# Split weights of the sorted experts made in two passes, the second on ScalarE, and output products moved into the sorted stage

## The chip, the cores and the metric

One core of a Trainium2 chip runs the whole program. The metric is the device time of one execution in microseconds (us). TensorE, VectorE, ScalarE, GpSimd and SyncE run their own instruction streams in order and wait for one another by semaphores; in the views they are PE (PEld for its weight loads), DVE, ACT, POOL and SP.

## What is computed

Sixteen batches of 256 tokens with 128 features go through an attention layer, whose attention matrix also drives a two-layer graph network, and then through a mixture of experts in which each token takes the best two of eight:

```python
attn = softmax(mask(q @ k.T))
out = attn @ v
adj = clip(attn + eye, 0, 1); deg = adj.sum(-1, keepdims=True)
feats = v
for l in range(2):
    feats = gelu(adj @ (feats @ gnn_w[l] + gnn_b[l]) / deg + feats)
x = x + layer_norm((out + feats @ lin_w + lin_b) @ Wo)
...
gate, up = split(normed @ gate_up_weight[e].T)     # 352 columns each, 8 experts
x = x + alpha * sum_e combine[e] * ((silu(gate) * up) @ down_weight[e].T)
```

The last sum runs over the two experts that each token chose.

## The kernel before

**Attention and graph network.** The sixteen batches are worked one after the other by a function `batch` on each engine; batches 0, 1 and 15 are written out, 2 to 14 are a loop. In a batch eight pairs of heads n are worked in a staggered order. That order is written by hand on each engine, as is every wait; nothing is scheduled by a program. One pair's path is: scores on TensorE; `maxima` on VectorE (L1406); `exps` on ScalarE (L1124) into `ea` and `eb`; `adjacency` on VectorE (L1418, L1421), four operations that take the larger of the weights and a scaled identity, with two inputs in SBUF; `weights` on VectorE (L1430); `graph` on GpSimd (L497, L499), which scales `ea` and `eb`; `degrees` on GpSimd (L508); the transposes on TensorE; their copies `gt` on ScalarE; and `differences`, whose result VectorE turns into `aT` (`difference`, `attended`) and ScalarE copies to `gvT`. Then the two graph layers: TensorE's product, VectorE's sum into `z` (`layer1_out`, `layer2_out`, L1455 and L1461), ScalarE's `gelu1`, `gelu2` and the copy `g`. The output products `output_attended` and `output_graph` gather in `bank[7]`; a batch's last seven are made in the next batch, and for batch 15 behind it, ahead of the sorted stage.

**Sorted experts.** Tokens are written to `slots` sorted by expert while later batches run; VectorE makes the table of steps in batch 15 (`table_first`: `passed_by`, `taken`, `used`). Then 71 steps follow, one tile of 128 tokens of one expert each. TensorE transposes the tile (L988), ScalarE and VectorE split it into a rounded high part and a low part (`sz_hi`, `sz_lo`), TensorE makes gate and up with three products for each (high by low, low by high, high by high), ScalarE takes silu, VectorE multiplies into `shid`, TensorE transposes and makes the down product. VectorE's `output_kept` (`y_now`) frees `bank[7]` of batch 15's output.

**The expert weights.** The gate and up weights need the same split, `gu_hi` and `gu_lo`, 128x704 for each of the eight experts. `gu_hi` lies where the attention weights were, so it cannot be written before the last `queries_keys` of batch 15. SyncE loads `raw_gu` into two buffers, the first two loads early and each next one when `gu_lo` of two experts earlier is made. In batch 15 VectorE casts (`gate_up_high`, L1468) behind each `layer2_out`, and GpSimd subtracts (`gate_up_low`, L539) after its last `degrees`.

Of the kernel before, what the change touches and what calls it, by code (L numbers as in the profile page):

```python
# [20 lines left out]
BATCHES, TOKENS, DIM = 16, 256, 128  # L21
# [51 lines left out]
def build_program(nc, x, wq, wk, wv, wvT, gnn_w, gnn_b, lin_wT, lin_b, wo, gamma_in, gamma_out,  # L73
# [10 lines left out]
    with ctx:  # L84
# [75 lines left out]
        gu_lo = sb("gu_lo", [P, EXPERTS, 2 * HID], f32r)  # L160

# [131 lines left out]
        k_gu_hi, k_gu_lo, w_out = sem("k_gu_hi"), sem("k_gu_lo"), sem("w_out")  # L293
# [42 lines left out]
        def _(sp):  # L336
# [95 lines left out]
        def _(pool):  # L432
# [109 lines left out]
            def batch(b, before, routed, after):  # L542

                graph(b, 0)
                degrees(b, 0)
                graph(b, 1)
                degrees(b, 1)
                graph(b, 2)
                degrees(b, 2)
                graph(b, 3)  # L550
                degrees(b, 3)
                graph(b, 4)
                graph(b, 5)
                degrees(b, 4)
# [7 lines left out]
                graph(b, 6)  # L562
                if routed is not None:
# [3 lines left out]
                graph(b, 7)  # L567
                degrees(b, 7)
                if after is not None:
                    deviation(after, 1, 7)  # L570
                if after is None:
                    for e in range(0, 3):
                        gate_up_low(e)
# [4 lines left out]
                if after is None:  # L578
                    for e in range(3, 5):
                        gate_up_low(e)  # L580
                if before is not None:
                    token_power(before, 2)
                if after is None:
                    for e in range(5, EXPERTS):
                        gate_up_low(e)
# [46 lines left out]
        def _(pe):  # L632
# [1425 lines left out]
```

## Time and profile before

| | us |
|---|---|
| median of 3 runs | 1147.88 |
| lowest and highest | 1142.15, 1152.14 |
| the profiled execution | 1155.31 |
| its span, first to last instruction | 1153.4 |

| engine | busy us | share of the span |
|---|---|---|
| TensorE, matmul | 1071.1 | 93% |
| TensorE, weight load | 854.7 | 74% |
| VectorE | 884.1 | 77% |
| ScalarE | 803.4 | 70% |
| GpSimd | 500.3 | 43% |

The profiled execution took 7.4 us more than the median. Batch 1, called the second batch here, runs from 84 to 142 us, the last batch from 898 to 955, the sorted stage from 957 to about 1135. A view by stage gives the busy time of each engine within a stretch and the clock that TensorE was granted; a timeline gives the start, the duration, the engine, the line and the tiles, with the idle time before it and what ended that in brackets. Durations of neighbouring instructions overlap a little, so the step from start to start is shorter than the duration.

### The profile page before, as it was taken

What the parts mean: (1) busy time and instruction counts of PE and PEld (TensorE: products, weight loads), DVE (VectorE), ACT (ScalarE), POOL (GpSimd) and SP (SyncE); (2) the same over time, 40 slices, a digit from 0 to 9 for tenths busy, and PEclk for the clock granted to TensorE, in tenths of its full rate; (3) what the DMA queues carried; (4) which work ended last, traced back from release to release, by engine and by line L of the source; (5) the groups of instructions that cost most, each with busy time, mean ns of one, the idle gap of its engine ahead of it and who ended that gap; (6) DMA issues with size and microseconds to landing.
All of it is one profiled execution on the core that took longest, in us unless ns stands there. A gap on an engine that the chain in (4) does not pass through costs nothing.

```text
span 1153.4 us, 28732 instructions
## 1 busy us (share of the span) xinstructions
PE 1071.1 (93%) x8576; PEld 854.7 (74%) x8576; DVE 884.1 (77%) x3760; ACT 803.4 (70%) x2351; POOL 500.3 (43%) x649
## 2 busy tenths in 40 slices
PE   4899999999999999999999999999999968898993
PEld 3777777777777777777777777777777747898993
DVE  3667797979797979797979797979797984565556
ACT  3668686868686868686868686868787735464551
POOL 3334244434343535353534353535353552544444
PEclk9899999999999999999999999999999988998997
DMA  6970000000000000000000000000000021222227
GB/s 192 405 260 2 1 2 11 1 10 1 10 1 11 1 10 0 10 0 10 0 10 0 10 0 10 0 10 0 10 0 10 2 78 44 56 57 61 59 61 226
DMA packets 37312, 47.43 MB, mean 41 GB/s; under 512 B 6009, under 2 KB 28539, under 8 KB 37200
## 3 DMA queue, kind: packets, MB, share of 16 engines
q1 hardware_dynamic: 32880, 37.81, 10.3%
q0 software_dynamic: 4320, 8.47, 2.2%
q14 instruction: 84, 0.69, 0.2%
q8 instruction: 28, 0.46, 0.2%
HBM read 18.14 MB, written 28.58 MB: 41 GB/s over the span
## 4 chain that ended last, share of the span: by engine, by line
PE 83%; DVE 6%; issue 3%; ACT 2%; SPq 2%; DMA 1%; another core or an unknown queue 1%; POOL 0%; DVEq 0%; POOLq 0%; ACTq 0%
PE bank L635 68%; PE bank L735 3%; PE bank L748 3%; PE bank L774 2%; PE bank L751 2%; PE bank L749 2%; PE bank L1006 2%; DMA x_all<-in_x 1%; PE bank L988 1%; DVE eb L1421 1%; DVE x_all L1995 1%; DVE got L1993 1%; DVE nmax L1406 0%; PE bank L783 0%
## 5 line engine op out<-in xcount | busy, mean ns | idle before, releaser
L497 POOL TENSOR_TENSOR ea<-ea,wgt 128x256 f32<-128x256 f32 x128 | 80.0, 625 | 429.6 <-DVE wgt L1430 396.1
L1406 DVE TENSOR_REDUCE nmax<-bank 128x1 f32<-128x128 f32 (+1 forms) x512 | 152.2, 347 | 66.0 <-PE bank L635 57.1
L499 POOL TENSOR_TENSOR eb<-eb,wgt 128x512 f32<-128x512 f32 x128 | 133.6, 1044 | 0.0
L635 PE MATMUL bank<-gt,g 128*64 128x256 f32 (+1 forms) x1024 | 112.0, 339 | 19.5 <-DVE z L1461 12.0
L1421 DVE SCALAR_TENSOR_TENSOR eb<-idw,ssum,eb 128x256 f32<-128x256 f32 x256 | 129.8, 544 | 0.0
L1124 ACT ACTIVATE ea<-bank,nmax 128x128 f32<-128x128 f32 x256 | 95.8, 374 | 47.9 <-DVE nmax L1406 45.9
L1124 ACT ACTIVATE eb<-bank,nmax 128x256 f32<-128x256 f32 x256 | 123.4, 482 | 0.0
L1092 ACT ACTIVATE gt<-bank 128x512 f32<-128x512 f32 (+1 forms) x256 | 111.7, 493 | 13.3 <-PE bank L751 11.8
L635 PE MATMUL bank<-gt,vnat 128*64 128x256 f32 (+1 forms) x1024 | 110.0, 335 | 3.0 <-issue 0.8
L635 PE MATMUL bank<-qk 64*128 64x128 f32 (+1 forms) x1024 | 112.7, 339 | 0.0
L525 POOL DMA_INDIRECT pairs<-zout,zin x71 | 69.7, 981 | 99.0 <-DVE zout L1954 89.3
L635 PEld LDWEIGHTS bank<-gt,g 128*64 128x64 f32 x1024 | 66.5, 137 | 61.4 <-issue 35.4
L1092 ACT ACTIVATE g<-bank 128x256 f32<-128x256 f32 x128 | 48.8, 381 | 84.8 <-PE bank L635 84.8
L635 PEld LDWEIGHTS bank<-gt,vnat 128*64 128x64 f32 x1024 | 65.1, 136 | 50.2 <-issue 17.0
L1461 DVE TENSOR_TENSOR z<-bank,f1T 128x256 f32<-128x256 f32 x128 | 53.6, 419 | 48.5 <-PE bank L635 48.5
L635 PE MATMUL bank<-xt_lo,w_hi 128*128 128x256 f32 x256 | 87.0, 340 | 1.9 <-DVE xt_lo L1399 1.9
L635 PE MATMUL bank<-gw,f1T 128*128 128x128 f32 x512 | 88.1, 295 | 0.3 <-ACT f1T L1148 0.3
L1947 DVE TENSOR_TENSOR shid<-bank,ssg 128x352 f32<-128x352 f32 x71 | 37.3, 525 | 63.5 <-ACT ssg L1272 40.6
L1092 ACT ACTIVATE qk<-bank 128x512 f32<-128x512 f32 x128 | 78.1, 610 | 11.2 <-PE bank L635 8.9
L635 PEld LDWEIGHTS bank<-gw,f1T 128*128 128x128 f32 x512 | 70.3, 192 | 19.3 <-issue 11.0
L1418 DVE SCALAR_TENSOR_TENSOR ea<-ident,ssum,ea 128x128 f32<-128x128 f32 x256 | 83.2, 362 | 0.0
L1092 ACT ACTIVATE gvT<-bank 128x256 f32<-128x256 f32 x128 | 49.1, 383 | 44.2 <-DVE aT L1440 40.6
(234 smaller groups left out, 3153.0 us busy)
## 6 DMA issues: line engine op xcount, KB each, us to landing
slots<-zero SPq DMA_DIRECT2D x33, 520.0 KB, 15.0
zin<-slots SPq DMA_DIRECT2D x71, 65.0 KB
got<-pairs SPq DMA_DIRECT2D x8, 512.0 KB, 5.5
raw_gu<-in_guT SPq DMA_DIRECT2D x8, 352.0 KB, 3.0
out<-x_all SPq DMA_DIRECT2D x8, 256.0 KB, 2.7
pairs<-zout,zin POOLq DMA_INDIRECT x71
dn<-in_downT SPq DMA_DIRECT2D x2, 512.0 KB, 16.0
slots<-z,row_now POOLq DMA_INDIRECT x64
```

What stands on the lines that cost most here:

```text
L497: nc.gpsimd.tensor_tensor(ea[:, s], ea[:, s], wgt[:, s, 0:2].unsqueeze(2).to_broadcast([P, 2, P]), ALU.mult)
L499: nc.gpsimd.tensor_tensor(eb[:, s], eb[:, s], wgt[:, s, 2:4].unsqueeze(2).to_broadcast([P, 2, 2 * P]), ALU.mult).then_inc(p_g.sem, 1)
L525: nc.gpsimd.indirect_dma_start(pairs, bass.IndirectOffsetOnAxis(ap=zin[:, j % RING, ID:ID + 1].bitcast(u32), axis=0), zout[:, j % RING, :] ...
L635: return nc_mm(o, st, mo, start=first, stop=last, **more)
L735: mm = nc.tensor.transpose(o[:, m * TOKENS + t * P:m * TOKENS + (t + 1) * P], vnat[:, t, n * P:(n + 1) * P], ident[:, :])
L1092: return nc.scalar.activation(o, i, ACT.Copy, **more)
L1124: done = nc.scalar.activation(e[:, s, a, :], score_bank(n, a)[:, TILE_SCORES[t]], ACT.Exp, bias=nmax[:, s, i:i + 1], accum_out=ssum[:, s, ...
L1406: done = V.tensor_reduce(nmax[:, n % 3, i:i + 1], score_bank(n, a)[:, TILE_SCORES[t]], X, ALU.max, negate=True)
L1418: V.scalar_tensor_tensor(ea[:, s, a, :], ident[:, :], ssum[:, s, a:a + 1], ea[:, s, a, :], ALU.mult, ALU.max, accum_out=den[:, s, a:a + 1])
L1421: done = V.scalar_tensor_tensor(eb[:, s, a, :], idw[:, :], ssum[:, s, 2 + a:3 + a], eb[:, s, a, :], ALU.mult, ALU.max, accum_out=den[:, s, ...
L1461: V.tensor_tensor(z2[:, n % 2, :], bank[L2_BANK][:, 0:TOKENS], f1T[:, n % 4, :], ALU.add).then_inc(d_z2.sem, 1)
L1947: V.tensor_tensor(shid[:, j % 2, 0:HID], bank[2 + j % 2][:, 0:HID], ssg[:, j % 2, :], ALU.mult).then_inc(d_hid.sem, 1)
```

## The change

The weight split is made in two passes. In the second batch VectorE casts the raw weights of expert e into `gu_top`, which lies in the buffer `zin` that the sorted stage uses later, right behind `weights(b, e)`; GpSimd subtracts it to make `gu_lo` right behind `graph(b, e)`, ahead of `degrees(b, e)`. There is one `gu_top`, so from the second expert on VectorE waits for GpSimd's subtraction before. All raw weights are then loaded a second time, and ScalarE casts them to `gu_hi` in the last batch, behind each `gelu1`. The seven last output products of batch 15 move behind the transposition of the sorted stage's first tile; `output_natural` and `output_kept` move from step 0 to step 1, the wait for `y_now` to step 2; and ScalarE calls a silu of one column ahead of the first slots, so that the table for silu is loaded there.

```diff
+        gu_top = zin[:, :, :].rearrange("p r d -> p (r d)")[:, 0:2 * HID].bitcast(f32r)
...
+            for e in range(EXPERTS):
+                if e < 2:
+                    sp.wait_ge(k_gu_lo, EXPERTS - 1 + e)
+                else:
+                    sp.wait_ge(k_gu_hi, e - 1)
+                sp.dma_start(raw_gu[:, e % 2, :], guT[e]).then_inc(w_gu[e % 2], 16)
...
             def gate_up_low(e):
-                pool.wait_ge(k_gu_hi, e + 1)
-                nc.gpsimd.tensor_tensor(gu_lo[:, e, :], raw_gu[:, e % 2, :], gu_hi[:, e, :].bitcast(f32),
+                pool.wait_ge(k_gu_top, e + 1)
+                nc.gpsimd.tensor_tensor(gu_lo[:, e, :], raw_gu[:, e % 2, :], gu_top.bitcast(f32),
                                         ALU.subtract).then_inc(k_gu_lo, 1)
...
+            def output_rest():
+
+                output_attended(BATCHES - 1, 5)
+                output_attended(BATCHES - 1, 6)
+                output_graph(BATCHES - 1, 4)
+                output_graph(BATCHES - 1, 5)
+                output_graph(BATCHES - 1, 6)
+                output_graph(BATCHES - 1, 7)
+                output_attended(BATCHES - 1, PAIRS - 1)
...
                 slots_transposed(0)
+                output_rest()
                 d_zlo.wait(pe, 0, 1)
                 slots_transposed(1)
...
                 pe.wait_ge(k_gu_lo, EXPERTS)
+                pe.wait_ge(k_gu_hi, EXPERTS)
...
-                    if j == 0:
+                    if j == 1:
                         output_natural(last)
+                    if j == 2:
                         d_y.wait(pe, last, 1)
...
+            def gate_up_high(e):
+                act.wait_ge(w_gu[e % 2], 16 * ((EXPERTS + e) // 2 + 1))
+                if e == 0:
+                    s_qk.wait(act, BATCHES - 1, PAIRS)
+                copy(gu_hi[:, e, :], raw_gu[:, e % 2, :]).then_inc(k_gu_hi, 1)
...
             def sorted_stage():
+                nc.scalar.activation(warm[:, :], half[:, 0:1], ACT.Silu)
                 slots_high(0)
...
-            def gate_up_high(e):
+            def gate_up_top(e):
                 dve.wait_ge(w_gu[e % 2], 16 * (e // 2 + 1))
-                if e == 0:
-                    s_qk.wait(dve, BATCHES - 1, PAIRS)
-                V.tensor_copy(gu_hi[:, e, :], raw_gu[:, e % 2, :]).then_inc(k_gu_hi, 1)
+                if e >= 1:
+                    dve.wait_ge(k_gu_lo, e)
+                V.tensor_copy(gu_top, raw_gu[:, e % 2, :]).then_inc(k_gu_top, 1)
...
                 slots_low(0)
+                output_bias(BATCHES - 1)
                 slots_low(1)
-                output_bias(BATCHES - 1)
...
-                    if j == 0:
+                    if j == 1:
                         output_kept(BATCHES - 1)
```

GpSimd at the start of the second batch, pairs 0 and 1, before (`ea` and `eb` are the scaled attention weights, `deg` the degrees):

```order
L497 TENSOR_TENSOR ea<-ea,wgt 128x256
L499 TENSOR_TENSOR eb<-eb,wgt 128x512
L508 TENSOR_TENSOR deg<-den,rs 128x256
L497 TENSOR_TENSOR ea<-ea,wgt 128x256
L499 TENSOR_TENSOR eb<-eb,wgt 128x512
L508 TENSOR_TENSOR deg<-den,rs 128x256
```

and in the changed kernel, where `zin` is the name of the buffer in which `gu_top` lies:

```order
L504 TENSOR_TENSOR ea<-ea,wgt 128x256
L506 TENSOR_TENSOR eb<-eb,wgt 128x512
L546 TENSOR_TENSOR gu_lo<-raw_gu,zin 128x704
L515 TENSOR_TENSOR deg<-den,rs 128x256
L504 TENSOR_TENSOR ea<-ea,wgt 128x256
L506 TENSOR_TENSOR eb<-eb,wgt 128x512
L546 TENSOR_TENSOR gu_lo<-raw_gu,zin 128x704
L515 TENSOR_TENSOR deg<-den,rs 128x256
```

One subtraction of 704 columns stands in each pair between `eb` and `deg`; for all eight pairs it is so.

VectorE at the same place in the changed kernel, from the `weights` of pair 0 (`wgt`) to the cast behind that of pair 1; before, the same rows stood without the two casts to `zin`:

```order
L1473 RECIPROCAL wgt<-den 128x4
L1511 CAST zin<-raw_gu 128x704
L1449 TENSOR_REDUCE nmax<-bank 128x1 x4
L1459 RECIPROCAL rs<-ssum 128x4
L1461 SCALAR_TENSOR_TENSOR ea,den<-ident,ssum,ea 128x128 x2
L1464 SCALAR_TENSOR_TENSOR eb,den<-idw,ssum,eb 128x256 x2
L1473 RECIPROCAL wgt<-den 128x4
L1511 CAST zin<-raw_gu 128x704
```

The cast stands between `wgt` and the maxima of the next pair, and the adjacency's four operations follow those.

ScalarE in the last batch of the changed kernel, around the second and third `gelu1` (`f1T`), where before the same rows stood without the casts to `gu_hi`:

```order
L1112 ACTIVATE gt<-bank 128x256
L1168 ACTIVATE f1T<-z,gb 128x256
L1112 ACTIVATE gu_hi<-raw_gu 128x704
L1112 ACTIVATE gvT<-bank 128x256
L1168 ACTIVATE f1T<-z,gb 128x256
L1112 ACTIVATE gu_hi<-raw_gu 128x704
L1112 ACTIVATE g<-bank 128x256 x2
L1112 ACTIVATE gt<-bank 128x512
```

These are the casts of experts 1 and 2; that of expert 0 stands two rows ahead of these, behind the first `f1T`. The copies `g`, for which the second layer's products wait, stand behind the third cast.

## Rows read from the trace of the kernel before

**Rows 1.** Busy time by stage: stretch, its length, busy of PE, PEld, DVE, ACT, POOL, clock.

```profile
84.00:142.00 58.00, 56.58 (x473) 43.82 (x471) 44.00 (x195) 45.20 (x135) 20.93 (x29) 1.00 0.01 1
926.00:955.00 29.00, 18.86 (x110) 13.40 (x107) 23.80 (x56) 8.78 (x22) 16.54 (x15) 0.76 0.31 86
```

**Rows 2.** The chain that ended last, in order of time: start, us, what.

```profile
926.20 4.40 DVE passed_by L1837
...
944.97 0.43 DVE gu_hi L1468
```

**Rows 3.** The tile `raw_gu`: durations in ns min/median/max, first and last start.

```profile
L1468 DVE CAST gu_hi<-raw_gu x8: 511/516/527, 923.5 to 953.9; 128x704 fp32r<-128x704 f32 x8
L539 POOL TENSOR_TENSOR gu_lo<-raw_gu,gu_hi x8: 1655/1672/1786, 928.8 to 954.5; 128x704 fp32r<-128x704 f32 x8
...
DMA to landing us min/median/max: 2.9/3.0/6.9
```

**Rows 4.** Timeline of the last batch, VectorE and GpSimd.

```profile
922.23 0.42 DVE L1813 TENSOR_TENSOR taken<-used,tile_to 128x256 f32<-128x256 f32 x1
...
928.85 1.66 POOL L539 TENSOR_TENSOR gu_lo<-raw_gu,gu_hi 128x704 fp32r<-128x704 f32 x1
...
942.26 1.67 POOL L539 TENSOR_TENSOR gu_lo<-raw_gu,gu_hi 128x704 fp32r<-128x704 f32 x1 [2.28 <-DVE gu_hi L1468]
...
942.36 1.86 DVE L1702 TENSOR_TENSOR x_all<-x_all,t 128x256 f32<-128x256 f32 x1
...
946.12 1.07 DVE L1713 TENSOR_SCALAR ve<-ss 128x2 f32<-128x2 f32 x1
...
948.20 1.78 DVE L1813 TENSOR_TENSOR taken<-used,tile_from 128x256 f32<-128x256 f32 x1
```

**Rows 5.** Timeline of the second batch, three engines.

```profile
118.58 1.04 POOL L499 TENSOR_TENSOR eb<-eb,wgt 128x512 f32<-128x512 f32 x1
118.64 1.13 DVE L1418 SCALAR_TENSOR_TENSOR ea<-ident,ssum,ea 128x128 f32<-128x128 f32 x1
...
122.65 1.66 DVE L1668 TENSOR_SCALAR t<-y_now,mv,rs 128x128 f32<-128x128 f32 x2
...
125.97 0.87 PE L635 MATMUL bank<-gt,g 128*64 128x256 f32 x8 [1.18 <-DVE z L1461]
```

**Rows 6.** Timeline of VectorE in the second batch.

```profile
95.41 0.18 DVE L1430 RECIPROCAL wgt<-den 128x4 f32<-128x4 f32 x1
...
98.13 0.32 DVE L1418 SCALAR_TENSOR_TENSOR ea<-ident,ssum,ea 128x128 f32<-128x128 f32 x1
...
99.80 0.17 DVE L1430 RECIPROCAL wgt<-den 128x4 f32<-128x4 f32 x1
...
121.80 0.16 DVE L1430 RECIPROCAL wgt<-den 128x4 f32<-128x4 f32 x1
```

**Rows 7.** Timeline of GpSimd in the second batch: start, us, instruction, [idle before].

```profile
95.67 0.61 POOL L497 TENSOR_TENSOR ea<-ea,wgt 128x256 f32<-128x256 f32 x1 [2.60 <-DVE wgt L1430]
96.24 1.04 POOL L499 TENSOR_TENSOR eb<-eb,wgt 128x512 f32<-128x512 f32 x1
97.24 0.61 POOL L508 TENSOR_TENSOR deg<-den,rs 128x256 f32<-128x256 f32 x1
```

**Rows 8.** TensorE's granted clock behind its long wait, columns as in the first group.

```profile
931.50:933.00 1.50, 1.50 (x9) 0.86 (x9) 1.02 (x6) 0.29 (x1) 1.24 (x1) 0.50 0.77 225
```

**Rows 9.** The tile `w_hi`: ScalarE's cast of it, durations in ns.

```profile
L1092 ACT ACTIVATE w_hi<-raw x2: 1056/1056/1057, 5.4 to 6.9; 128x1024 fp32r<-128x1024 f32 x2
```

**Rows 10.** Timeline of TensorE before the long wait of the last batch.

```profile
919.90 0.82 PE L635 MATMUL bank<-gt,g 128*64 128x256 f32 x8
```

**Rows 11.** Timeline of the first steps of the sorted stage.

```profile
959.12 0.42 PE L635 MATMUL bank<-gu_lo,sz_hi 128*128 x1
...
959.46 1.28 ACT L1272 ACT_TABLE_LOAD   x1
...
963.04 0.42 PE L635 MATMUL bank<-gu_lo,sz_hi 128*128 x1 [2.33 <-DVE y_now L1448]
```

More of the change, by code:

```diff
@@ L537, in gate_up_low @@
             def gate_up_low(e):
-                pool.wait_ge(k_gu_hi, e + 1)
-                nc.gpsimd.tensor_tensor(gu_lo[:, e, :], raw_gu[:, e % 2, :], gu_hi[:, e, :].bitcast(f32),
+                pool.wait_ge(k_gu_top, e + 1)
+                nc.gpsimd.tensor_tensor(gu_lo[:, e, :], raw_gu[:, e % 2, :], gu_top.bitcast(f32),
                                         ALU.subtract).then_inc(k_gu_lo, 1)
             def batch(b, before, routed, after):
+                first_pass = before is not None and routed is None
                 graph(b, 0)
+                if first_pass:
+                    gate_up_low(0)
                 degrees(b, 0)
                 graph(b, 1)
+                if first_pass:
+                    gate_up_low(1)
                 degrees(b, 1)
                 graph(b, 2)
+                if first_pass:
+                    gate_up_low(2)
                 degrees(b, 2)
                 graph(b, 3)
+                if first_pass:
+                    gate_up_low(3)
                 degrees(b, 3)
                 graph(b, 4)
+                if first_pass:
+                    gate_up_low(4)
                 graph(b, 5)
+                if first_pass:
+                    gate_up_low(5)
                 degrees(b, 4)
@@ L1211, in batch @@
                 gelu1(b, 0)
+                if after is None:
+                    gate_up_high(0)
                 graph(b, 5)
                 gelu1(b, 1)
+                if after is None:
+                    gate_up_high(1)
                 mixed_values(b, 4)
                 gelu1(b, 2)
+                if after is None:
+                    gate_up_high(2)
                 layer2_in(b, 0)
@@ L1221, in batch @@
                 gelu1(b, 3)
+                if after is None:
+                    gate_up_high(3)
                 gelu2(b, 0)
                 gelu1(b, 4)
+                if after is None:
+                    gate_up_high(4)
                 gelu2(b, 1)
@@ L1227, in batch @@
                 gelu1(b, 5)
+                if after is None:
+                    gate_up_high(5)
                 layer2_in(b, 4)
@@ L1232, in batch @@
                 gelu1(b, 6)
+                if after is None:
+                    gate_up_high(6)
                 layer2_in(b, 5)
@@ L1239, in batch @@
                 gelu1(b, 7)
+                if after is None:
+                    gate_up_high(7)
                 layer2_in(b, 7)
@@ L1548, in batch @@
                 layer2_out(b, 0)
-                if after is None:
-                    gate_up_high(0)
                 weights(b, 7)
+                if first_pass:
+                    gate_up_top(7)
                 difference(b, 5)
@@ L1563, in batch @@
                 layer2_out(b, 1)
-                if after is None:
-                    gate_up_high(1)
                 if before is not None:
@@ L1572, in batch @@
                 layer2_out(b, 2)
-                if after is None:
-                    gate_up_high(2)
                 difference(b, 6)
@@ L1596, in batch @@
                 layer2_out(b, 4)
-                if after is None:
-                    gate_up_high(4)
                 difference(b, 7)
@@ L1605, in batch @@
                 layer2_out(b, 5)
-                if after is None:
-                    gate_up_high(5)
                 layer1_out(b, 7)
```

43 lines of the change are left out of this document (20 added, 23 removed).

## The prediction

> **What bounds the kernel now.** I read the profile in this order: the busy time by stage, the chain that ended last, the timeline of the second batch, the timeline of the last batch, and the first steps of the sorted stage.
>
> In the second batch (from 84 to 142 us) TensorE is busy 56.58 of 58 us at a full granted clock, VectorE 44.00 and GpSimd 20.93 [rows 1]. TensorE is the bound there, and there is hardly any idle time to lose anything in. In the end of the last batch (926 to 955 us) TensorE is busy 18.86 of 29 us at a mean granted clock of 0.76 and VectorE 23.80 [rows 1]. There VectorE is the bound, and the chain says so: it runs through 4.40 us of `passed_by` and through casts to `gu_hi`, each 0.43 us of it [rows 2]. So the change takes VectorE and GpSimd work from a place where it is on the path, and puts it where TensorE is the bound and has no room. What it costs there decides.
>
> **What the second batch pays.** Eight VectorE casts of 128x704 and eight GpSimd subtractions of the same size go in. A cast takes 516 ns and a subtraction 1672 ns [rows 3]; of the cast 0.43 us stand in the chain [rows 2], the rest overlaps with its neighbours. Summed alone that is 3.4 us on VectorE and 13.4 us on GpSimd, and GpSimd is busy 20.93 of 58 us, so by busy time it would fit.
>
> It does not fit by position. VectorE's operations with two SBUF inputs wait while GpSimd works. In the last batch the 128x64 `passed_by`, in the chain from 926.20 for 4.40 us [rows 2], ended 0.1 us after a subtraction that began at 928.85 and took 1.66; a 128x256 addition to `x_all` took 1.86 us beside a subtraction that began 0.10 us before it; `ve` on 128x2 took 1.07 us, and `taken` 1.78 us against 0.42 for the same form undisturbed [rows 4]. In the second batch the same happens once to the adjacency: an `ea` of 128x128 took 1.13 us, beside a GpSimd `eb` that ended at 119.62 [rows 5], against 0.32 us for one that met nothing [rows 6].
>
> Now the cycle of one pair n there. `weights` ends at 95.59 [rows 6], GpSimd starts 0.08 us later and does `ea`, `eb`, `deg` until 97.85 [rows 7]; the next adjacency begins at 98.13 and its `weights` at 99.80 [rows 6]. The adjacency just misses GpSimd, by 0.28 us. From the second `weights` at 95.41 to the eighth at 121.80 [rows 6] there are six periods, of 4.40 us in the mean. After the change, counted from the end of `weights`: the cast, first in VectorE's order, holds GpSimd back by about 0.3 us; `ea` and `eb` take 0.57 and 1.00 us from start to start [rows 7], the subtraction about 1.64, `deg` 0.57. The subtraction thus ends at 0.1 + 0.3 + 1.57 + 1.64 = 3.6 us and `deg` at 4.2. The next adjacency, due at about 2.5 to 3.0, waits to 3.6. It does one of its four operations (0.25 us), waits for `deg` to 4.2, and does the rest. From its first operation to the next `weights` is 99.80 - 98.13 = 1.67 us now [rows 6], so 4.2 + 1.42 + 0.1 = 5.7 us to the next `weights`, against 4.4. Over seven periods that is 7 x 1.3 = 9.1 us. Behind the last `weights` two normalisations, now 1.66 us with a wait, meet the eighth subtraction too, about 1.6 us more, and TensorE already waits there for VectorE, 1.18 us [rows 5], so this comes through in full. That makes 10.7. I take off 1.7, an estimate, for the first periods, in which VectorE idles for TensorE now: **+9.0 us**. TensorE waits for `gvT` and `z`, both behind the late operations in VectorE's order, and since it is 98% busy it makes nothing good later.
>
> The ends of this price: below, if adjacency and subtraction never meet, only the casts remain, and these partly in idle time: +2 us. Above, if a waiting operation is not let in between two GpSimd instructions (`passed_by` stood behind the whole queue of them), each adjacency waits for `deg` whole, 0.35 us more a period, and nothing is taken off, +13 us. I take the value in between since the `ea` of 1.13 us, the same operation, was let in at the end of `eb`, before `deg`.
>
> The Trainium skill says the same of the mechanism: by "SBUF — State Buffer", section "Who interferes with whom", VectorE and GpSimd share one port pair under an exclusive lock, an instruction of VectorE with two SBUF inputs contends with a GpSimd instruction that reads SBUF, and whoever issues first holds it for its whole instruction. By that rule a waiting operation comes in when the instruction that holds the ports ends, which is the period of 5.7 us and the 9.0; the `ea` of 1.13 us agrees, and `passed_by`, which stood behind several instructions, goes further than the rule and would give the 13.
>
> The raw weights are loaded twice now, eight more transfers of 352 KB. A load lands in 3.0 us [rows 3] and has two periods of over 4 us; that costs nothing in the second batch. GpSimd's `degrees` and powers come up to 1.7 us later; inside the 9.0.
>
> **What the last batch gains.** (a) `passed_by` is released when GpSimd's queue ends without the first subtraction, 928.9 instead of 930.5: **-1.7 us**, as TensorE waits for the `z` behind it. (b) From 937 us to 951 us the chain is VectorE's. Gone are the waits of `x_all` (1.86 to 0.42), `ve` (1.07 to 0.17) and `taken` (1.78 to 0.42) [rows 4], the short times of the first two by their widths, 3.7 us, and three casts of 0.43 us, 1.3 us. With VectorE 5.0 us faster the round from `z2` through TensorE and ScalarE becomes the limit, so I let 1.3 us of it go and count **-3.7 us**. (c) TensorE's granted clock is 0.50, the lower level of 1.2 GHz, at 931.5 to 933 us [rows 8], behind its long idle stretch; its busy part on the chain there is slower than at 2.4 GHz. With that stretch shorter some of it comes back; 0 to 4 us, I take **-1.5 us**.
>
> ScalarE gets eight casts of 128x704. A 128x1024 one took 1056 ns [rows 9], so about 0.79 us each, 6.3 us in all; ScalarE is busy 8.78 of 29 us at the end [rows 1], which hides the last five. The first three stand in a crowded place. The third needs a load that can start only when the first has released its buffer, at about 918.3 us by my estimate, and lands 3.0 us later [rows 3]; ScalarE stands in front of it until 921.3, and `layer2_in` behind it, for which TensorE's `gt,g` products, at 919.90 now [rows 10], wait until about 922.4. That 2.5 us is covered by the wait for `passed_by` until 928.9, and TensorE idles 10 of the 29 us there [rows 1]. Cost nothing; 2.5 us if that cover is gone.
>
> **What the sorted stage gains.** The two slot conversions on ScalarE and VectorE now run under the seven moved products, but a table load of 1.28 us [rows 11] now stands before the first conversion: -0.7 us. Between step 0 (959.12) and step 1 TensorE waits 2.33 us for `y_now` [rows 11]. With the table loaded before and the wait two steps later, step 1 follows directly and the transposition behind it costs nothing: -2.1 us. Together **-2.8 us**, from nothing to 4 us. All later stalls of the stage hang on its step numbers and shift with it.
>
> **Sum.** +9.0 - 1.7 - 3.7 - 1.5 - 2.8 = -0.7 us on the profiled execution, which took 1155.31 us. The median of the timed runs is 1147.88 us, 7 below it, so the sum is put on the median: 1147.2 us.
>
> **Rivals.**
> 1. The port is not the limit in the second batch (+2 us instead of +9). For it: VectorE idles there 14 us by busy time. Against it: the 0.28 us by which the adjacency clears GpSimd now. 1147.9 - 9.7 + 2 = 1140 us.
> 2. Slower: TensorE's waits in the second batch, 1 to 2 us in each period, bring its clock to the lower level as behind the idle stretch at 926 us, and the batch becomes slow on TensorE too. For it: 0.50 at 931.5 [rows 8]. It decides when the clock is down for over 8 us of the batch, since half of that is lost: +4 to +8. Against it: its waits are broken up by work. With `deg` waited for whole it gives 1147.9 + 13 + 4 - 9.7 = 1155 us.
> 3. The gain of the last batch does not come: ScalarE's third cast delays the queue by 2.5 us with no cover, and TensorE's chain is the limit anyway, so that (a) to (c) bring 2 us rather than 6.9: 1152 us.
>
> **How the numbers follow.** The forecast has 0.48, rival 1 has 0.24, rival 2 has 0.14, rival 3 has 0.14. The likeliest gives 1147.2 us, with 1143 to 1151 as its own range. The whole range, to rivals 1 and 2 and their bounds, is 1138 to 1157 us. A measurement of this kernel tells about 1% from no change: under 1136.4 all gains at their upper bounds and the cheap second batch must meet, 0.07; over 1159.4 rival 2 must meet the failing gains, 0.08; 0.85 lies within.
>
> **What would show it.** In the second batch: `weights` to `weights` at 5.7 us, `ea` and `eb` of VectorE over 1 us at each pair, TensorE waiting several times. If `ea` stays at 0.32 to 0.35 us there, the term of 9.0 us is wrong. In the last batch: `passed_by` under 3 us, `x_all`, `taken` and `ve` at their short times, and ScalarE waiting for a load ahead of its third cast. In the sorted stage: no wait for `y_now`, and step 2 about 3.2 us after step 0. A batch two that ends more than 13 us late, or a clock below 1.00 in it, would make the forecast too low.

## The result and the profile after

| | before | after |
|---|---|---|
| median of 6 runs each, us | 1147.82 | 1162.82 |
| lowest and highest | 1142.15, 1152.14 | 1160.69, 1165.88 |
| span of the profiled execution | 1153.4 | 1161.9 |

The ratio is 1.0131, with a 95% interval of 1.0100 to 1.0161: the change costs 15 us. The forecast of 1147.2 us is wrong, and the range, which ended at 1157, too.

Four stretches of the trace that can be cut at the same events in both kernels say where the time went. I cut at the first `weights` of a batch (VectorE's reciprocal into `wgt`), at the first gate and up product and at the last transposition of a hidden tile.

| stretch, us | before | after | difference |
|---|---|---|---|
| second batch, to the first `weights` of batch 2 | 56.9 | 67.5 | +10.6 |
| batches 2 to 14, to the first `weights` of batch 15 | 742.7 | 759.2 | +16.5 |
| last batch, to the first gate and up product | 69.0 | 58.1 | -10.9 |
| sorted stage, to its last transposition | 175.8 | 168.1 | -7.7 |

The differences add up to 8.5 us and not to the 15 of the medians, since the profiled execution of before took 7.4 us more than its median. The first, the third and the fourth are what the prediction was about. The second was in no sentence of it: in the loop of batches 2 to 14 no line was changed, and it costs 16.5 us more, the size of the whole loss. Of the fourth only a part is the change's, as the runs below show.

The views by stage, the second batch first, then the last. The columns are start and end of the stretch, its length, the busy time of each engine with its instructions, TensorE's granted clock, and the DMA share and rate.

```profile
core 0: us, PE busy (x) PEld busy (x) DVE busy (x) ACT busy (x) POOL busy (x), PEclk, DMA share, GB/s
90.50:158.00 67.50, 57.96 (x457) 44.34 (x456) 56.47 (x208) 44.39 (x132) 35.84 (x37) 0.97 0.15 44
917.20:975.30 58.10, 51.66 (x415) 39.03 (x413) 48.58 (x198) 44.56 (x127) 23.88 (x31) 1.00 0.20 52
```

For the same two stretches of the kernel before:

```profile
90.60:147.50 56.90, 55.48 (x459) 42.89 (x458) 44.56 (x201) 43.92 (x133) 20.93 (x29) 1.00 0.01 2
890.10:959.10 69.00, 56.65 (x415) 42.46 (x412) 57.84 (x206) 37.75 (x118) 37.23 (x39) 0.90 0.16 44
```

In the second batch GpSimd has 15 us more and VectorE 12 us more, of which only some 4 us are casts. In the last batch VectorE lost 9 us and GpSimd 13, and TensorE's clock is at its full level (2.4 GHz) throughout, where it was 0.90 in the mean.

How the second batch loses, from the timelines of GpSimd and then of VectorE in the kernel after (start, duration, engine, line, operation, tiles; in brackets the idle time before and what ended it):

```profile
96.86 1.03 POOL L506 TENSOR_TENSOR eb<-eb,wgt 128x512 f32<-128x512 f32 x1
97.85 1.68 POOL L546 TENSOR_TENSOR gu_lo<-raw_gu,zin 128x704 fp32r<-128x704 f32 x1
99.49 0.66 POOL L515 TENSOR_TENSOR deg<-den,rs 128x256 f32<-128x256 f32 x1
...
101.62 0.80 POOL L504 TENSOR_TENSOR ea<-ea,wgt 128x256 f32<-128x256 f32 x1 [1.47 <-DVE wgt L1473]
```

```profile
98.06 1.62 DVE L1461 SCALAR_TENSOR_TENSOR ea<-ident,ssum,ea 128x128 f32<-128x128 f32 x1
99.61 0.08 DVE L1461 DVE_READ_ACCUMULATOR ea<-ident,ssum,ea 128x1 f32 x1
99.61 0.69 DVE L1461 SCALAR_TENSOR_TENSOR ea<-ident,ssum,ea 128x128 f32<-128x128 f32 x1
```

The first `ea` of this pair, 0.32 us long in [rows 6], starts 0.21 us behind the subtraction and ends 0.15 us behind it; the second takes 0.69 us and ends 0.15 us behind `deg`. GpSimd's `ea` of the eight pairs begin at 90.82 to 129.53 us, a period of 5.53 us.

How the loop loses. This is VectorE's timeline at the jump from one pass to the next in the kernel after, and then at the same jump in the kernel before:

```profile
383.60 0.43 DVE L1504 TENSOR_TENSOR z<-bank,f1T 128x256 f32<-128x256 f32 x1 [1.94 <-PE bank L650]
386.81 0.62 DVE L1449 TENSOR_REDUCE nmax<-bank 128x1 f32<-128x128 f32 x2 [2.78 <-PE bank L650]
389.27 0.62 DVE L1449 TENSOR_REDUCE nmax<-bank 128x1 f32<-128x128 f32 x2 [1.84 <-issue]
389.81 0.17 DVE L1773 COPY lg<-bank 128x16 f32<-128x16 f32 x1
```

```profile
369.12 0.42 DVE L1461 TENSOR_TENSOR z<-bank,f1T 128x256 f32<-128x256 f32 x1 [1.95 <-PE bank L635]
372.13 1.15 DVE L1406 TENSOR_REDUCE nmax<-bank 128x1 f32<-128x128 f32 x4 [2.58 <-PE bank L635]
373.19 0.17 DVE L1729 COPY lg<-bank 128x16 f32<-128x16 f32 x1
...
374.59 0.17 DVE L1737 MAX8 top<-lg 128x8 f32<-128x8 f32 x1 [0.35 <-issue]
```

Before, four reductions follow one another (and a small stand of 0.35 us comes 18 instructions behind the head). After, VectorE does two, then stands still for 1.84 us with nothing to wait for ("issue"), and then does the other two of the four. Over all passes, VectorE's waits of after and then TensorE's (in all, times, the longest):

```profile
DVE nmax L1449 <- issue: 23.7, 13, 2.8
```

```profile
PE bank L650 <- DVE lg L1773: 8.9, 12, 0.9
PE bank L750 <- ACT vnat L1112: 3.3, 12, 0.3
```

The loop jumps back twelve times. VectorE's 13 waits are the twelve second stands and once the first one. TensorE waits 0.7 us in the mean for `lg` in each of twelve passes, and 0.3 us for `vnat`; for neither it waited before. From jump to jump a pass takes 58.49 us in the mean against 57.12, 1.37 us more. An engine that stands still at one place in its code, on no semaphore, in every pass, may be waiting for the code itself. The DMA queues on the page show code being read (packets, MB, share), after first:

```profile
q14 instruction: 86, 0.70, 0.2%
q8 instruction: 28, 0.46, 0.2%
```

```profile
q14 instruction: 84, 0.69, 0.2%
q8 instruction: 28, 0.46, 0.2%
```

Their number hardly differs, so it is not that more is read. What differs is when it is needed. In the trace VectorE has 429 instructions ahead of the loop's head before and 444 after: the eight casts and seven waits of the change make it 15 later. The packets of queue 14 are of 8192 bytes (0.70 MB in 86). In both traces a packet of this queue begins 1.0 to 1.2 us behind the jump of VectorE's loop shown, and the next one 0.8 us after VectorE goes on. The theory to test, called P: VectorE's code comes in blocks; behind the jump the block with the head is read, and then the next; after the change only three instructions of the loop stand in the first of them.

### The profile page after: what moved, and what is told of

The parts are those of the page before. It is cut to its first block, busy times and chain, and to the rows that moved or that the text cites. A ratio compares the mean times of both kernels' runs of the same rounds, so it can differ in the third digit from the quotient of the medians.

```text
span 1161.9 us, 28757 instructions
## 1 busy us (share of the span) xinstructions
PE 1073.4 (92%) x8576; PEld 853.1 (73%) x8576; DVE 890.8 (77%) x3760; ACT 812.3 (70%) x2360; POOL 501.4 (43%) x649
## 4 chain that ended last, share of the span: by engine, by line
PE 62%; DVE 19%; issue 10%; DMA 3%; ACT 3%; SPq 2%; POOL 1%; DVEq 1%; ACTq 0%; POOLq 0%
PE bank L650 49%; DVE eb L1464 4%; PE bank L750 3%; DVE nmax L1449 3%; DVE ea L1461 2%; PE bank L789 2%; PE bank L763 2%; DVE z L1498 2%; PE bank L766 2%; PE bank L764 2%; PE bank L1021 2%; DVE z L1504 1%; DMA zin<-slots 1%; DVE dT L1478 1%; DVE t L1712 1%
## 5 line engine op out<-in xcount | busy, mean ns | idle before, releaser
L1461 DVE SCALAR_TENSOR_TENSOR ea<-ident,ssum,ea 128x128 f32<-128x128 f32 x256 | 89.9, 388 | 0.0
```

The lines of the kernel that those rows point to most:

```text
L1461: V.scalar_tensor_tensor(ea[:, s, a, :], ident[:, :], ssum[:, s, a:a + 1], ea[:, s, a, :], ALU.mult, ALU.max, accum_out=den[:, s, a:a + 1])
```

## Experiments

Twelve kernels ran. Times are medians in us, and each group was timed beside the kernel before on its own chip, which differs by up to 8 us from group to group; so only differences and ratios within a group are compared. "The good place" means that VectorE's loop head stands near the start of a block.

| run | time | before beside it | ratio, 95% interval |
|---|---|---|---|
| before, head 15 later | 1168.61 | 1153.38 | 1.0148 (1.0122 to 1.0174) |
| after, head 2 later | 1177.53 | 1153.38 | 1.0215 (1.0185 to 1.0245) |
| after, head 4 later | 1151.68 | 1153.38 | 0.9993 (0.9974 to 1.0013) |
| before with the sorted part | 1148.46 | 1153.38 | 0.9955 (0.9936 to 0.9974) |
| after, head 4 later, subtractions of 2 columns | 1134.90 | 1146.12 | 0.9886 (0.9853 to 0.9919) |
| after, head 4 later, without the sorted part | 1147.86 | 1146.12 | 1.0011 (0.9999 to 1.0023) |
| after, subtractions on VectorE | 1139.22 | 1146.12 | 0.9941 (0.9924 to 0.9959) |
| before with the sorted part, head 19 later | 1140.85 | 1146.12 | 0.9958 (0.9943 to 0.9972) |
| before, head 19 later | 1142.59 | 1145.31 | 0.9981 (0.9964 to 0.9998) |
| the same with the sorted part and ScalarE's casts | 1137.35 | 1145.31 | 0.9927 (0.9911 to 0.9944) |
| after, head 94 later | 1145.88, one run | 1145.31 | |
| after, head 102 later | 1145.0, one run | 1145.31 | |

### Does the place of the loop's head make the 16 us?

The first kernel is before with 15 idle instructions on VectorE ahead of its first wait; each EVENT_SEMAPHORE holds two waits that are satisfied.

```diff
+            for _ in range(30):
+                dve.wait_ge(w_x0, 16)
             dve.wait_ge(w_x0, 16)
             for i in range(5):
```

> The kernel before, with 15 more instructions on VectorE ahead of its first wait: each waits for a semaphore that has its value anyway. Nothing else changes; the loop of batches 2 to 14 stands 15 instructions later in VectorE's code, as in the kernel after. Theory P (place of the loop's head in the code): in the trace of the kernel after, VectorE stands still 1.7 us behind the third instruction of every pass, on no semaphore, and a pass takes 58.5 us against 57.1; so this kernel must show the same stall and passes of 58.4 to 58.6 us, and be 13 x 1.3 = about 16 us slower, 1164 us. Theory C (the second batch's casts and subtractions, or what follows from them, slow the loop down): this kernel has none of them, passes stay at 57.1 us and the time at 1148.

It took 15.2 us more than before, ratio 1.0148, with nothing of the change in it. Its trace at the jump, and its wait over all passes:

```profile
375.94 0.62 DVE L1406 TENSOR_REDUCE nmax<-bank 128x1 f32<-128x128 f32 x2 [2.56 <-PE bank L635]
378.38 0.62 DVE L1406 TENSOR_REDUCE nmax<-bank 128x1 f32<-128x128 f32 x2 [1.82 <-issue]
```

```profile
DVE nmax L1406 <- issue: 23.3, 13, 2.9
```

This is the stall of after at the same instruction, and a pass takes 58.44 us. The second batch keeps its 56.8 us there, so its casts and subtractions are not needed for the slow loop. The other way round, the kernel after with 2 and with 4 more (`range(8)` in the second):

```diff
+            for _ in range(4):
+                dve.wait_ge(w_x0, 16)
             dve.wait_ge(w_x0, 16)
```

> The kernel after with 2 more such instructions on VectorE ahead of its first wait. Theory P with code read in blocks of 128 instructions: the head then stands 1 instruction ahead of a block's end instead of 3, the stall stays, behind the first instruction instead of the third; pass 58.4 us or a little more, time 1163 us. Theory C: no change, 1163 us. It is the partner of the next kernel, which has 2 more.

> The kernel after with 4 more such instructions. Theory P: the loop's head passes the end of a block, so that 127 instructions of the loop are in the first block read behind the jump; the stall of 1.7 us is gone, a pass takes 57.0 us or a little less, and the time is 1163 - 13 x 1.3 to 1.6 = 1142 to 1147 us. Theory C: 1163 us, as the one with 2.

With 2 it is 24 us slower than before, with 4 it is 1.7 us faster than before: two idle instructions are worth 26 us. VectorE's timeline with 2, then with 4:

```profile
385.61 0.43 DVE L1504 TENSOR_TENSOR z<-bank,f1T 128x256 f32<-128x256 f32 x1 [1.94 <-PE bank L650]
391.20 1.15 DVE L1449 TENSOR_REDUCE nmax<-bank 128x1 f32<-128x128 f32 x4 [5.16 <-issue]
```

```profile
379.41 0.43 DVE L1504 TENSOR_TENSOR z<-bank,f1T 128x256 f32<-128x256 f32 x1 [1.94 <-PE bank L650]
381.67 1.15 DVE L1449 TENSOR_REDUCE nmax<-bank 128x1 f32<-128x128 f32 x4 [1.83 <-PE bank L650]
```

With 2 the second stall has moved up to the second instruction, as the theory said. But a pass takes 59.19 us, more than the 58.4 that I had written, and the kernel is 24 us over before where the expectation meant 15; both stands together are 5.16 us, and no reduction of the pass is done between them. Whether that makes the additional 0.7 us of a pass was not tested. With 4 both stalls are gone. VectorE waits 1.83 us for TensorE and for nothing else; a pass takes 57.00 us, and the profile shows

```profile
q14 instruction: 26, 0.21, 0.1%
```

26 packets instead of 86. I had expected that the stall would go, not that all reading would stop. So VectorE can hold the whole loop, but only from some places. Two more kernels test a rule for that, with 94 and with 102 idle instructions.

> The kernel after with 94 more satisfied waits ahead: the loop's head is instruction 90 of its block (from 0), the jump at its end 288 further, in the third block. If four blocks of 128 are held and one is fetched ahead, the block of the head is still there when the loop jumps: no fetch of code in the loop, about 26 packets in the instruction queue, 0.2 us behind the jump. Time as the one with 4, if the waits ahead cost nothing.

> The same with 102: head at 98, the jump in the fourth block, so the next one was fetched over the head's. Fetches in every pass again (84 to 86 packets), 2.7 to 2.9 us from the jump to the next instruction, but no second stall, as 30 instructions are in the first block read. Time within 2 us of the one with 94.

Both came out as written, the times from one run each. The queue and VectorE's timeline with 94, and then with 102:

```profile
q14 instruction: 27, 0.22, 0.1%
```

```profile
381.23 0.43 DVE L1504 TENSOR_TENSOR z<-bank,f1T 128x256 f32<-128x256 f32 x1 [1.94 <-PE bank L650]
383.49 1.15 DVE L1449 TENSOR_REDUCE nmax<-bank 128x1 f32<-128x128 f32 x4 [1.83 <-PE bank L650]
```

```profile
q14 instruction: 87, 0.71, 0.2%
```

```profile
381.53 0.43 DVE L1504 TENSOR_TENSOR z<-bank,f1T 128x256 f32<-128x256 f32 x1 [1.94 <-PE bank L650]
384.51 1.15 DVE L1449 TENSOR_REDUCE nmax<-bank 128x1 f32<-128x128 f32 x4 [2.55 <-PE bank L650]
```

With blocks of 128, a block border ahead of instruction 447 (counted from 0) fits all places: after (head at 444) stalls behind three instructions, with 2 more behind one, and before (429) has its small stand behind 18. With 4 more the head is at 448, one behind the border by this count, not the block's first as I had written, and the jump 288 instructions further is in the third block, counted from the head's; with 94 (538) it is still in the third, with 102 (546) in the fourth. The packets fit a store of four blocks into which the next one is read ahead: with the jump in the fourth block, as also in before and after, the head's block has been written over. This store is worked out from which places read and which don't; no view shows it.

The reading alone costs nothing here: with 102 a pass takes 56.99 us, and with 94, where nothing is read, 56.99 too. At 429 the 18 loop instructions ahead of the border cover the reading of the next block but for 0.35 us. So three cases were seen: no reading; reading whose 2.6 us hide under VectorE's wait for TensorE; and, with 3 or 1 instructions left in the head's block, a second stall that does not hide. How many instructions between 3 and 18 are enough was not tried.

The Trainium skill has this mechanism in "Runtime: NRT & Kernel Launch", section "Instruction fetch mechanics": a taken branch to a page outside the window makes the engine wait for a DMA that brings it. The trace agrees in kind. The page speaks of blocks of 256 instructions; here the measurement decides, and eight kilobytes and 128 instructions fit for VectorE. With borders every 256 instructions through the same 447 the jump of the kernel with 102 would be in the block next to its head's, and it reads in every pass.

What the better place gives a kernel that already had no second stall:

> The kernel before with 19 more satisfied waits ahead, so that the loop's head is the first instruction of a block. Theory P: a pass takes 57.0 us without the spread of 56.95 to 57.66 that the profile of before shows, and the fetches in the loop are gone: 13 x 0.12 = 1.6 us at most, 1144.5 to 1146 us where before is 1146. So the other kernels with this place of the head have at most 1.6 us from it.

2.7 us by the medians, where at most 1.6 was expected; the interval of 0.9964 to 0.9998 (0.2 to 4.1 us) takes that in. A pass takes 56.98 us there, without the slow ones up to 57.66. The loop's stretch in the traces bounds it better: 742.7 us in before, 741.4 in the kernel with the sorted part alone, which has its head at the same place, and 741.1 here. So the good place is worth 0.3 to 1.6 us against that of before.

### What is the change worth without that?

The kernel after with 4 more is the change at a good place: 0.9993 of before, or -0.8 us with -3.0 to +1.5, where the prediction's sum was -0.7. But before stands at a slightly worse place; against before at the good one (0.9981, in another group) it is 1.0012, +1.4 us, with about -1.6 to +4.4 by both intervals together. Either way the change is nothing that these runs can tell from zero. Its parts:

> The kernel before with the sorted stage's part of the change alone: seven output products behind the first transposition, output_natural and output_kept one step later, the wait for y_now two steps later, the table of silu loaded ahead. VectorE's code ahead of the loop is that of before, so passes stay at 57.1 us. By the prediction's term -2.8 us: 1145 us. By the two traces, in which the stretch from the first gate and up product to the last hidden transposition shrank by 7.7 us, up to -7.7 us: 1140 us. If most of that 7.7 us comes from the earlier end of the last batch's work instead (weights split ready earlier), 1145 to 1147 us.

```diff
+                output_rest()
...
-                    if j == 0:
+                    if j == 1:
                         output_natural(last)
+                    if j == 2:
                         d_y.wait(pe, last, 1)
...
+                nc.scalar.activation(warm[:, :], half[:, 0:1], ACT.Silu)
```

4.9 us by the medians (3.0 to 7.4 by the interval), and the wait for `y_now`, 2.33 us in [rows 11], is gone. At the good place the sorted part was run in another group:

> The sorted part alone (e4) with 19 more instructions ahead, which puts the loop's head at the same place as in e3, the first instruction of a block by my count. A pass is 57.00 us there against 57.02 in the profile of e4 and 57.12 in that of before. So it gives 0.2 to 1.5 us on top of e4: 1147 to 1148 us where before is 1153. The fetches of code in the loop disappear (26 packets in the instruction queue instead of 84).

0.9958 with it against 0.9981 without (above, on another chip): 0.23%, 2.6 us, beside a prediction of 2.8. The sorted stage's stretch of the table at the top took 171.3 and 161.3 us in the two kernels with the sorted part alone (head as before, and 19 later), and 168.7 in the one with 19 idle instructions and no sorted part. It moves by 10 us between two kernels, on two chips, that differ only in the place of the loop; in the one of 161.3 the granted clock was 1.00 over the whole stretch, in that of before 0.96. So a part of the -7.7 us of the two profiles is such a difference, and by the times 2.6 to 4.9 us are the change's.

The split of the weights alone, at the good place:

> The kernel after with 4 more instructions ahead, the sorted stage's part undone: the seven output products, output_natural, output_kept, the wait for y_now and silu's table stand as in the kernel before. The split of the weights in two passes is there. By the runs so far the whole change at the good place is -1.7 us and the sorted part alone -4.9, so by addition the split alone is +3 us against before: 1156 us where before is 1153. By the prediction's terms it is +9.0 - 6.9 = +2.1. If the sorted part's gain needs the earlier low parts (the stretch from the first gate and up product shrank by 7.7 us in the whole change), the split alone is worse, +6 us.

```diff
-                output_rest()
+            output_attended(BATCHES - 1, 5)
...
-                    if j == 1:
+                    if j == 0:
                         output_kept(BATCHES - 1)
```

+1.7 us, ratio 1.0011 with 0.9999 to 1.0023, against before at its own place, which is 0.3 to 1.6 us worse by the traces. The prediction's terms give +9.0 - 6.9 = +2.1. The two halves of the split largely cancel, and of the change as written the sorted part is the only clear gain.

### What costs the 10.6 us in the second batch?

> The kernel after with 4 more instructions ahead (the good place of the loop's head), and in the second batch GpSimd subtracts 2 columns of each expert instead of 704; the other columns of the low parts are zero, filled once by GpSimd at 17 us where it idles. So the low parts are left out but for 2 columns. VectorE's eight casts stay. If the second batch's price is GpSimd's 1.67 us holding VectorE's two-input operations, the batch gets back nearly all of its 10.7 us: 3 us at most are left for the casts, the period of weights is 4.4 to 4.6 us, and the time is 8 us under that of the partner with 4 (e3), about 1144 us where that is 1152. If the casts or the loads cost it, under 3 us come back.

```diff
-                nc.gpsimd.tensor_tensor(gu_lo[:, e, :], raw_gu[:, e % 2, :], gu_top.bitcast(f32),
+                nc.gpsimd.tensor_tensor(gu_lo[:, e, 0:2], raw_gu[:, e % 2, 0:2], gu_top[:, 0:2].bitcast(f32),
```

11.2 us under before by the medians, ratio 0.9886, so 12 us under its partner of 0.9993 where 8 were expected; its runs spread over 9 us, and the trace is the surer measure. The second batch takes 57.8 us: of the 10.6 us, 9.7 belong to GpSimd's subtraction and 0.9 to the eight casts and the loads. VectorE's first two adjacency operations of a pair in the second batch, and its casts, in the kernel after and then in this one (busy, mean ns):

```profile
L1461 DVE SCALAR_TENSOR_TENSOR ea<-ident,ssum,ea 128x128 f32<-128x128 f32 x16 | 12.6, 823 | 0.0
L1511 DVE CAST zin<-raw_gu 128x704 fp32r<-128x704 f32 x8 | 4.2, 527 | 0.0
```

```profile
L1463 DVE SCALAR_TENSOR_TENSOR ea<-ident,ssum,ea 128x128 f32<-128x128 f32 x16 | 5.4, 378 | 0.0
L1513 DVE CAST zin<-raw_gu 128x704 fp32r<-128x704 f32 x8 | 4.0, 499 | 0.0
```

823 against 378 ns for 16 of them is 7.1 us of waiting. Another 1.9 us stand in the normalisations of the same stretch: `t` (two of 1279 against 820 ns), `xh` (two of 490 against 335) and `ve` (804 against 168). One of them beside the subtraction, in after:

```profile
119.64 1.67 POOL L546 TENSOR_TENSOR gu_lo<-raw_gu,zin 128x704 fp32r<-128x704 f32 x1
120.54 0.80 DVE L1707 TENSOR_SCALAR ve<-mv 128x2 f32<-128x2 f32 x1
```

`ve` reads one tile, and it ends 0.03 us behind the subtraction. So it is not only operations with two inputs in SBUF that are held, as the prediction had it; its own example `ve` was of this kind. The last 0.7 us were not parted. Is it GpSimd, or would any engine cost as much?

> The kernel after with the low parts in the second batch made by VectorE, one step behind its cast, instead of by GpSimd. Its eight subtractions put the loop's head 8 or more instructions later, which is behind the block's end, so no padding. A subtraction of 128x704 with two SBUF inputs on VectorE is about 0.8 us by the width of the 128x1024 one of 1.22 us; 8 x 0.75 = 6 us more work for VectorE, which was idle 14 of 58 us in that batch. If only the lock made the 10.7 us, the second batch costs 2 to 6 us instead and the time is 5 to 9 us under that of the kernel with 4 (e3), 1143 to 1147 us where that is 1152. If VectorE's busy time is the limit then, as much as before, no gain.

```diff
+            def gate_up_low(e):
+                dve.wait_ge(k_gu_top, e + 1)
+                V.tensor_tensor(gu_lo[:, e, :], raw_gu[:, e % 2, :], gu_top.bitcast(f32),
+                                ALU.subtract).then_inc(k_gu_lo, 1)
...
                 maxima(b, 1, 1)
+                if first_pass:
+                    gate_up_low(0)
```

1139.22 against 1146.12, ratio 0.9941. Here are its operations in the second batch, and the batch as a whole:

```profile
L1493 DVE TENSOR_TENSOR gu_lo<-raw_gu,zin 128x704 fp32r<-128x704 f32 x8 | 7.9, 993 | 0.0
L1445 DVE SCALAR_TENSOR_TENSOR ea<-ident,ssum,ea 128x128 f32<-128x128 f32 x16 | 5.8, 401 | 0.0
```

```profile
90.80:153.30 62.50, 56.64 (x458) 43.12 (x456) 54.13 (x217) 43.87 (x132) 28.27 (x29) 1.00 0.16 48
```

The batch takes 62.5 us: with the eight casts, eight subtractions that each occupy VectorE for 0.99 us cost 5.6 us, where GpSimd's of 1.68 us cost 10.6. So the same subtraction costs less on the engine with more to do, and with VectorE's own `ea` is at 401 ns again, against 407 in before. That it also stands at another place in the pair's order was not tested apart.

### Which part of the last batch gains?

> The kernel e8 (sorted part, good place) in which ScalarE makes the high parts in the last batch instead of VectorE, and GpSimd still subtracts in the last batch, behind them; no second pass of loads, nothing in the second batch. ScalarE's casts from the third on stand somewhat later than in the kernel after, so that the loads they wait for can come. It parts the gain of the last batch, of which e3 has 10 to 11 us by its trace (from the first weights of the last batch to the first gate and up product, 69 to 58 us): if the casts on VectorE are what counts, this kernel shows 62 to 65 us there and is 3 us or more under e8; if it is GpSimd's subtractions, it stays at 66 to 70 us and the time is that of e8 within 2 us.

```diff
-            def gate_up_high(e):
-                dve.wait_ge(w_gu[e % 2], 16 * (e // 2 + 1))
...
+            def gate_up_high(e):
+                act.wait_ge(w_gu[e % 2], 16 * (e // 2 + 1))
+                if e == 0:
+                    s_qk.wait(act, BATCHES - 1, PAIRS)
+                copy(gu_hi[:, e, :], raw_gu[:, e % 2, :]).then_inc(k_gu_hi, 1)
...
                 gelu1(b, 0)
+                if after is None:
+                    gate_up_high(0)
```

1137.35 us, ratio 0.9927: the fastest of those that leave nothing out, 8.0 us under before; it is faster than before and after, each at its own place and at the good one. Its last stretch beside that of the kernel without ScalarE's casts (the sorted part, head 19 later):

```profile
888.30:954.50 66.20, 55.34 (x413) 41.64 (x412) 53.51 (x198) 44.74 (x127) 37.45 (x39) 0.92 0.16 46
```

```profile
888.90:957.90 69.00, 57.26 (x416) 42.89 (x414) 57.84 (x206) 38.99 (x119) 37.25 (x39) 0.90 0.16 44
```

In these two traces the casts' move gives 2.8 us of the stretch, and 66.2 us lies at the lower end of what was expected if the casts don't count (66 to 70, against 62 to 65 if they do). But the stretch varies with TensorE's clock: the five kernels with the old last batch have 66.8 to 70.3 us, the eight with the whole split 58.1 to 60.7. The clock was at its lower level for 10.2 us of the 66.2 and for 13.7 of the 69.0. The kernel with the sorted part and the head as before has 10.2 us of low clock too and 67.7 us, so at equal clock the casts' share is 1.5 us, from one trace each. The subtractions' removal is worth the rest, 5.5 to 8 us. The times have 0.9927 against 0.9958 without ScalarE's casts, in two groups: 3.6 us, and the intervals just touch. Moving casts and subtractions to the second batch costs 10.6 us there. So with GpSimd's subtractions in the second batch, only the half of the split that moved to ScalarE pays, and it pays little.

## Why the prediction was wrong, point by point

**The loop: the step that failed.** The sum went from the second batch to the last as if the thirteen batches between were safe, since none of their lines or waits changed. It holds no term for the position of the code. That term, put at nothing without a reason, is +16.5 us in the trace and +15.2 us measured by itself, and with it removed the kernel takes 0.9993 of before. The costs of the added instructions were counted as busy time and as waits, never as places in an instruction stream with a jump behind it. The hint was there: a page of before with 84 packets of code and VectorE idle for 2.6 us in front of the same reduction of each pass, where it idles 1.83 us when nothing is read.

**The second batch, +9.0.** +10.6. The mechanism came out as it was told: period 5.53 us where 5.7 was written, the first `ea` let in at the end of the subtraction, the second at the end of `deg` in the pair shown, and TensorE recovering nothing. The seven periods from `weights` to `weights` cost 7.6 us, as 9.1 less the 1.7 taken off says; the first costs 0.5 us, the last 1.9. The 1.6 us that are missing lie behind the eighth `weights`: 3.0 us where 1.6 was counted. TensorE's clock is at its lower level for 3.4 us there, which is worth up to 1.7 us of that, an estimate. Rule and row agree: by "SBUF — State Buffer" of the Trainium skill, section "Who interferes with whom", whoever holds the ports keeps them for one instruction, and 1.62 us of `ea` beside 1.68 us of `gu_lo` is that; the end of 13 us was not reached.

**The last batch, -6.9 with -0.7 from the conversions.** -10.9 us over both in these two traces, 3.3 us more than counted; over all kernels with the old and with the new last batch the means differ by 9.1 us, 1.5 more than counted. The signs are there: `x_all` takes 0.43 us, `ve` 0.16, `taken` 0.42. Two terms look too small. (a) let `passed_by` wait until 928.9 us, for -1.7. It doesn't wait at all; before and then after:

```profile
926.12 4.47 DVE L1837 TENSOR_TENSOR passed_by<-upto,tiles_full 128x64 f32<-128x64 f32 x1
931.39 1.55 PE L635 MATMUL bank<-gt,g 128*64 128x256 f32 x8 [5.10 <-DVE z L1461]
```

```profile
953.74 0.29 DVE L1881 TENSOR_TENSOR passed_by<-upto,tiles_full 128x64 f32<-128x64 f32 x1
956.02 0.87 PE L650 MATMUL bank<-gt,g 128*64 128x256 f32 x8 [1.97 <-DVE z L1504]
```

TensorE's wait behind it is 3.1 us shorter. It is in part chance: the kernel with the sorted part alone, whose last batch is unchanged, has a `passed_by` of 0.30 us too, and its stretch is still 67.7 us. (c), TensorE's clock: 0.90 over the stretch before, 13.7 us at the lower level of 1.2 GHz, is 1.00 after. I had given it 1.5 of its 0 to 4 us. The kernels give an estimate: with the old last batch, 6.8 us of low clock go with 66.8 us, and 13.7 with 68.9 to 70.3; with the split, none with 58.1, and 3.4 with 59.5 to 60.7. At 0.4 to 0.5 us for each, the 13.7 us are worth 5 to 7. That would be the whole excess, if the low clock is the cause and does not just come with a longer idle stretch of TensorE. No run parts (a), (b) and (c). ScalarE's third cast waited 0.37 us for its load, as told, and cost nothing that shows.

**The sorted stage, -2.8.** Between 2.6 and 4.9 us in two comparisons; right.

**The rivals.** None of them held the case. Rival 1 fell with the period of 5.53 us. Of rival 2 a trace is there, 3.4 us at the lower clock level from 135.3 us on, worth at most 1.7 us; 8 us of low clock were needed. Rival 3 fell with 58.1 us. All four cases lay within 1140 to 1155 us since all shared the loop that doesn't change.

**The sum.** At the good place the change measured -0.8 us and the sum said -0.7, but that is partly luck: the second batch cost 1.6 us more than counted, the last batch gave 1.5 to 3.3 us more, and before itself stands at a place up to 1.6 us worse.

## What to carry to other kernels

Whoever adds or removes instructions ahead of a loop should count them on each engine, and compare in the trace the time behind the loop's jump and the packets in the instruction queues. A stall put down to "issue" at the same instruction in every pass may be code being read, as it was on VectorE here, where packets of an instruction queue begin in it. The label alone doesn't show it: TensorE has a wait of 0.6 us put down to "issue" in each pass also in the kernel with 4, where VectorE's loop reads nothing. A few idle instructions ahead of the loop can be worth more than the change itself. Before a change is judged, its time should be taken at two places of the code. And work for GpSimd should be placed by what VectorE does meanwhile: a subtraction of 1.68 us beside VectorE's adjacency cost 1.2 us in each period here (9.7 us in eight), while the same subtraction on VectorE cost half of that (4.7 us in eight).

## What the hardware showed that I had not expected

- Two idle instructions move this kernel from 1177.53 to 1151.68 us.
- VectorE's loop of 289 traced instructions is read anew in each pass or not at all, by the place of its head alone (27 packets in the whole run with 94 idle instructions, 87 with 102). The first block is there about 3 us behind the jump. The next one is asked for only then: in the profile of after, at the jump of 383.7 us, the packets of queue 14 begin at 384.9 and 387.6 us, and VectorE goes on at 386.7 and 389.3. So the fewer instructions are left in the first block, the less of the second reading they cover; with 3 left the second stand ends about 2.5 us behind the first.
- ScalarE's and GpSimd's loops, 187 and 50 traced instructions, stood for 0.2 and 0.1 us at their jumps in the same traces.
